# Cross attention with an RWKV block: recurrence over pairs of tokens, tail with channels on partitions, gate as silu on ScalarE

## The reference

```python
xa = _ln(x, ln1_w, ln1_b)
sx = concatenate([state[:, 1:2] - xa[:, :1], xa[:, :-1] - xa[:, 1:]], axis=1)
xxx = tanh((xa + sx * maa_x) @ maa_w1)            # five mixes of xa and sx from it
w = exp(-exp(time_decay + tanh(xw @ td_w1) @ td_w2))
r, k, v = xr @ Wr.T, xk @ Wk.T, xv @ Wv.T         # 32 heads of 16 channels
g = silu(xg @ Wg.T)
def step(s, rkvw):                                # over the 128 tokens
    a = k_t[..., :, None] * v_t[..., None, :]
    out = einsum('bhi,bhij->bhj', r_t, u * a + s)
    s = a + w_t[..., :, None] * s
og = (out - mean) / sqrt(var + 1e-05)             # per head
x1 = x + (og * gn_w + gn_b) * g @ Wo.T
# then a second layer norm and a channel mixing with Wfk, Wfr, Wfv on x1
```

## Time and profile before

| | |
|---|---|
| median of 3 runs | 1902.09 us (1901.77 to 1902.61) |
| the profiled execution's own time | 1903.22 us |
| its span | 1901.3 us |
| mean granted clock of TensorE | 0.976 of 2.4 GHz |
| TensorE, VectorE busy | 1761.4, 1775.5 us |
| ScalarE, GpSimd busy | 1196.1, 1253.3 us |

### The profile page before, as it was taken

The page is one execution under the profiler, slowest core; times in us unless marked ns, Lnnn a source line. Parts: engine busy times, 40 slices in busy tenths (PEclk is TensorE's granted clock), DMA queues, the critical chain, the costliest instruction groups (busy, mean ns, idle before and its releaser), DMA issues.

```text
span 1901.3 us, 34866 instructions
## 1 busy us (share of the span) xinstructions
PE 1761.4 (93%) x12356; PEld 1228.6 (65%) x12356; DVE 1775.5 (93%) x2084; ACT 1196.1 (63%) x2849; POOL 1253.3 (66%) x822
## 2 busy tenths in 40 slices
PE   5888999999999999999999999999999999999866
PEld 3666676767666677766667776666776666676533
DVE  3599999999999999999999999999999999999981
ACT  3546666666666666666666666666666666666422
POOL 1246777676777767677777766777776677776541
PEclk8899999999999999999999999999999999999878
DMA  6233433333343333333333443333443333333320
GB/s 239 60 98 96 106 102 92 101 104 102 100 106 99 92 101 104 104 101 102 99 91 102 106 106 98 103 98 91 105 107 103 98 103 96 95 107 96 91 66 11
DMA packets 86203, 189.32 MB, mean 100 GB/s; under 512 B 18800, under 2 KB 35312, under 8 KB 85008
## 3 DMA queue, kind: packets, MB, share of 16 engines
q1 hardware_dynamic: 64528, 170.32, 33.7%
q10 hardware_dynamic: 21504, 16.78, 2.7%
HBM read 161.91 MB, written 16.78 MB: 94 GB/s over the span
## 4 chain that ended last, share of the span: by engine, by line
DVE 52%; issue 24%; POOL 11%; PE 7%; ACT 6%; DVEq 0%; DMA 0%; POOLq 0%; ACTq 0%; SPq 0%
DVE S L615 18%; DVE S L606 8%; DVE S L624 8%; POOL rstd L402 7%; ACT wrep L863 3%; DVE xf L578 3%; PE bank L1004 3%; DVE nmax L521 3%; DVE xx L568 2%; PE bank L1011 1%; DVE xin L531 1%; POOL rstd L400 1%; DVE st L663 1%; DVE x L659 1%; POOL S L446 1%
## 5 line engine op out<-in xcount | busy, mean ns | idle before, releaser
L615 DVE TENSOR_TENSOR_SCAN S<-wrep,S 128x1024 f32<-128x1024 f32 x256 | 602.6, 2354 | 2.1 <-ACT wrep L863 0.8
L446 POOL COPY S<-s 128x8 f32<-128x8 f32 x256 | 281.4, 1100 | 291.9 <-PE bank L1129 283.3
L624 DVE TENSOR_TENSOR S<-S,rT 128x1024 f32<-128x1024 f32 x256 | 343.3, 1341 | 2.8 <-ACT rT L868 1.6
L606 DVE TENSOR_TENSOR S<-vrep,kT 128x1016 f32<-128x1016 f32 x256 | 341.0, 1332 | 0.0
L430 POOL TENSOR_TENSOR xf<-xf,xa 128x512 f32<-128x512 f32 x160 | 249.3, 1558 | 89.8 <-DVE xf L578 87.5
L402 POOL TENSOR_TENSOR rstd<-rstd,mhalf 128x1 f32<-128x1 f32 (+1 forms) x96 | 211.3, 2201 | 8.0
L1129 PE MATMUL bank<-S,slide 128*32 128x256 f32 x2048 | 165.0, 394 | 23.8 <-DVE S L624 23.7
L827 ACT ACTIVATE bank<-bank,par 128x128 f32<-128x128 f32 x640 | 175.8, 366 | 10.6 <-PE bank L1085 10.6
L402 POOL TENSOR_TENSOR hrs<-hrs,mhalf 128x32 f32<-128x32 f32 x32 | 174.8, 5462 | 2.7
L400 POOL TENSOR_SCALAR rstd<-mv 128x1 f32<-128x1 f32 (+1 forms) x96 | 36.2, 377 | 204.9 <-DVE mv L542 151.8
L790 ACT ACTIVATE prob<-bank,nmax 128x512 f32<-128x512 f32 x128 | 88.3, 690 | 102.4 <-DVE nmax L521 101.5
(11 more groups left out here) (131 smaller groups left out, 3763.3 us busy)
## 6 DMA issues: line engine op xcount, KB each, us to landing
vrep<-v_dram SPq DMA_DIRECT2D x256, 512.0 KB
xc<-x_c SPq DMA_DIRECT2D x32, 256.0 KB, 6.4
xs<-x_s SPq DMA_DIRECT2D x32, 256.0 KB, 7.1
v_dram<-vT ACTq DMA_DIRECT2D x32, 256.0 KB, 2.3
xres<-xin SPq DMA_DIRECT2D x32, 256.0 KB, 6.1
out<-rr ACTq DMA_DIRECT2D x32, 256.0 KB, 2.0
Wv<-big_w SPq DMA_DIRECT2D x1, 1024.0 KB, 7.3
Wk<-big_w SPq DMA_DIRECT2D x1, 1024.0 KB, 9.3
```

What stands on the lines that cost most here:

```text
L446: po.tensor_copy(S[:, u % 2, :, 0], s0[:, p, k:k + UJ]).then_inc(pool_wkv.sem, 1)
L606: ve_.tensor_tensor(S[:, u % 2, :, 1:P], vrep[:, u % 2, :, 0:P - 1], k, ALU.mult).then_inc(dve_wkv.sem, 1)
L615: ve_.tensor_tensor_scan(s, wrep[:, u % C, :, :].rearrange("p j t -> p (j t)"), s, 0.0, ALU.mult, ALU.add).then_inc(dve_wkv.sem, 1)
L624: ve_.tensor_tensor(s, s, rT[:, p, u % C, :].unsqueeze(1).broadcast_to([P, UJ, P]), ALU.mult).then_inc(dve_wkv.sem, 1)
```

## The change

1. **Pairs of tokens.** With s(t+2) = w w' s(t) + (w' a + a'), the scan goes over the state before every even token: 64 per row in place of 128. Into k of the even tokens goes the next token's decay (`mid_kw`), into r of the odd tokens the even token's decay (`mid_rw`); `wkv_pair` adds the two products; the read multiplies each state with both tokens' r. The even token's own product, which the odd token's output needs, goes in through a second bonus: r of the odd with k of the even token (`wkv_rk2`), summed per head on TensorE (`tail_C`) and multiplied with the even token's v (`tail_o2`, `tail_ob`). GpSimd multiplies the two decays (`mid_ez2`); ScalarE computes w once (`mid_w`), and `decay` becomes a repeated copy of 504 elements per chunk.
2. **Tail with channels on partitions.** The columns of Wv and Wg and the rows of Wo are reordered on the host, so that the sums of the recurrence lie like v and the gate. `tail_To` and `tail_Tg` and the copy of the sums go; `tail_os` adds the sums to the bonus from PSUM. The variance is a product with a block of ones (`tail_Vr`), epsilon is added on ScalarE (`tail_hv`), the power stays on GpSimd, its result is repeated (`tail_hp`), transposed (`tail_Rs`), and multiplied in from PSUM (`tail_gn`).
3. **Gate.** `mid_th` is silu from its bank, `mid_gate` goes. The activations need more than one function table, so loads of a table are placed between them.
4. **Around it.** xin has three buffers and the copy to xres goes. v is stored by four transfers. The back jobs have three banks. kT and rT lose their second buffer, kt and rt have two. All five orders are new.

```diff
+            def mid_ez2(n, m, p):
+                eng.wait_ge(act_mid.sem, act_mid.count("dw", n))
+                eng.wait_ge(act_decay.sem, act_decay.count("w3", n - 1))
+                po.tensor_tensor(ez2[:, :, :], first(ez[:, :, :]), second(ez[:, :, :]), ALU.mult).then_inc(pool_ez2.sem, 1)
...
+            def wkv_rk2(n, m, p):
+                eng.wait_ge(act_mid.sem, act_mid.count("r", n))
+                eng.wait_ge(pe_tail.sem, pe_tail.count("C", n - 1))
+                po.tensor_tensor(rk2[:, :, :], second(rT[:, :, :]), first(kT[:, :, :]), ALU.mult).then_inc(pool_rk2.sem, 1)
...
+                ve_.tensor_tensor(first(kt[:, p, :, :]), first(kT[:, :, :]), second(ez[:, :, :]),
+                                  ALU.mult).then_inc(dve_pre.sem, 1)
...
+                k = kt[:, p, u % C, 0:P - 2].unsqueeze(1).broadcast_to([P, UJ, P - 2])
+                ve_.tensor_tensor(A[:, u % 2, :, 0:P - 2], vrep[:, u % 2, :, 0:P - 2], k, ALU.mult).then_inc(dve_outer.sem, 1)
+
+            def wkv_pair(n, m, p, u):
+                eng.wait_ge(dve_outer.sem, dve_outer.count(f"a{u}", n))
+                a = A[:, u % 2, :, 0:P - 2]
+                ve_.tensor_tensor(S[:, u % 2, :, 1:T2], first(a), second(a), ALU.add).then_inc(dve_pair.sem, 1)
...
+                out4 = A[:, u % 2, :, :].rearrange("p j (m k) -> p j m k", k=2)
+                s = S[:, u % 2, :, :].unsqueeze(3).broadcast_to([P, UJ, T2, 2])
+                r = rt[:, p, u % C, :].rearrange("p (m k) -> p m k", k=2).unsqueeze(1).broadcast_to([P, UJ, T2, 2])
+                ve_.tensor_tensor(out4, s, r, ALU.mult).then_inc(dve_read.sem, 1)
...
+            def tail_os(n, m, p):
+                eng.wait_ge(dve_tail.sem, dve_tail.count("ob", n))
+                eng.wait_ge(pe_wkv.sem, pe_wkv.count(f"r{U - 1}", n))
+                ve_.tensor_tensor(oc[:, :], bank[SUM_BANK][:, :], oc[:, :], ALU.add).then_inc(dve_tail.sem, 1)
...
+                for g in range(P // H):
+                    eng.dma_start(rows[g], vT[H * g:H * (g + 1), p, :, :]).then_inc(v_stored, 16)
...
-                sc.activation(wrep[:, c, :, 1:P], ez[:, c, 0:P - 1].unsqueeze(1).broadcast_to([P, UJ, P - 1]),
-                              ACT.Exp, scale=-1.0).then_inc(act_decay.sem, 1)
+                sc.activation(wrep[:, c, :, 1:T2], ez2[:, c, 0:T2 - 1].unsqueeze(1).broadcast_to([P, UJ, T2 - 1]),
+                              ACT.Copy).then_inc(act_decay.sem, 1)
...
-                sc.activation(gT[:, p, :, :], by_chunk(bank_of("G")[:, :]), ACT.Tanh, scale=0.5).then_inc(act_mid.sem, 1)
+                sc.activation(gT[:, p, :, :], by_chunk(bank_of("G")[:, :]), ACT.Silu).then_inc(act_mid.sem, 1)
...
+                for c in range(C):
+                    last = pe.matmul(bank_of("C")[:, P:P + T2], heads_of[:, c, :], rk2[:, c, :],
+                                     start=(c == 0), stop=(c == C - 1))
...
+            def tail_Vr(n, m, p):
+                eng.wait_ge(act_tail.sem, act_tail.count("sq", n))
+                eng.wait_ge(*bank_free("Vr", n))
+                for c in range(C):
+                    last = pe.matmul(bank_of("Vr")[:, 0:H], sq[:, c * P:(c + 1) * P], head_sum[:, :],
+                                     start=(c == 0), stop=(c == C - 1))
```

More of the change, by code:

```diff
@@ L31 @@
 U = C * HS // UJ
-CONSTS = 14 + C
+T2 = P // 2
+CONSTS = 16 + 3 * C
 LAGS = 5
@@ L179, in by_chunk, with first, second @@
             return ap.rearrange("p (c t) -> p c t", c=C)
+        def first(ap):
+            return ap.rearrange("p c (m k) -> p c m k", k=2)[:, :, :, 0]
+        def second(ap):
+            return ap.rearrange("p c (m k) -> p c m k", k=2)[:, :, :, 1]
         xn = prob[:, 0, :]
@@ L549, in centre_wv @@
                 eng.wait_ge(setup_loaded[2], 16 * len(BIG))
-                wv = W["Wv"][:, :, :].rearrange("p c (h j) -> p (c h) j", j=HS)
-                total = sx[:, 0, :]
+                wv = W["Wv"][:, :, :].rearrange("p c (j h) -> p c h j", j=HS)
+                total = sx[:, 0, :].rearrange("p (c h) -> p c h", c=C)
                 ve_.tensor_reduce(total, wv, X, ALU.add).then_inc(wv_centred, 1)
                 eng.wait_ge(wv_centred, 1)
-                ve_.scalar_tensor_tensor(wv, total.unsqueeze(2).broadcast_to([P, C * H, HS]), -1.0 / HS, wv,
-                                         ALU.mult, ALU.add).then_inc(wv_centred, 1)
+                for c in range(C):
+                    last = ve_.scalar_tensor_tensor(wv[:, c, :, :], total[:, c, :].unsqueeze(2).broadcast_to([P, H, HS]),
+                                                    -1.0 / HS, wv[:, c, :, :], ALU.mult, ALU.add)
+                last.then_inc(wv_centred, 1)
                 eng.wait_ge(wv_centred, 2)
@@ new lines, in tail_ob @@
+            def tail_ob(n, m, p):
+                eng.wait_ge(dve_tail.sem, dve_tail.count("o2", n))
+                b2 = second(by_chunk(oc[:, :]))
+                ve_.tensor_tensor(b2, b2, pv[:, :, :], ALU.add).then_inc(dve_tail.sem, 1)
+            def tail_os(n, m, p):
+                eng.wait_ge(dve_tail.sem, dve_tail.count("ob", n))
+                eng.wait_ge(pe_wkv.sem, pe_wkv.count(f"r{U - 1}", n))
+                ve_.tensor_tensor(oc[:, :], bank[SUM_BANK][:, :], oc[:, :], ALU.add).then_inc(dve_tail.sem, 1)
@@ L755, in step @@
-                if b1: wkv_outer(*b1, 0)
             run(step)
@@ L1149, in tail_To, with tail_Rs @@
                 for c in range(C):
-                    last = pe.matmul(bank[O_BANK][:, c * P:(c + 1) * P], bonus[:, c * P:(c + 1) * P], ident[:, :],
-                                     start=False, stop=(c == C - 1), is_transpose=True)
+                    last = pe.matmul(bank_of("Vr")[:, 0:H], sq[:, c * P:(c + 1) * P], head_sum[:, :],
+                                     start=(c == 0), stop=(c == C - 1))
                 last.then_inc(pe_tail.sem, 1)
-            def tail_Tg(n, m, p):
-                eng.wait_ge(dve_tail.sem, dve_tail.count("o3", n))
-                eng.wait_ge(*bank_free("Tg", n))
-                transposes("Tg", lambda c: oc[:, c * P:(c + 1) * P]).then_inc(pe_tail.sem, 1)
+            def tail_Rs(n, m, p):
+                eng.wait_ge(act_tail.sem, act_tail.count("hp", n))
+                eng.wait_ge(*bank_free("Rs", n))
+                pe.transpose(bank_of("Rs")[:, 0:P], hrep[:, :], ident[:, :]).then_inc(pe_tail.sem, 1)
```

483 lines of the change are left out of this document (263 added, 220 removed).

## The result

The changed kernel took 1906.7 us, median of 10 runs (1905.4 to 1911.2), beside 1901.9 for the kernel before on the same chip: ratio 1.0029, 95% interval 1.0019 to 1.0039. It is slower by 0.3%, where 1882 was forecast. The profiled execution took 1906.4 us; its span is 3.4 us longer than that of the kernel before.

A forecast was written before the change was run, and what follows sets the result against it. VectorE was taken to bound the kernel before, TensorE after the change. Thirty periods at 0.59 us gave 18 us, the ends 2, the profiled execution 1: 1903.2 - 20 - 1 = 1882 us, range 1855 to 1926.

The forecast's parts named there:

- TensorE's work: TensorE per period: transposes out, bonus and variance products in, 53.82 to 53.95 us (53.7 to 54.6), becoming the bound.
- VectorE's need: VectorE per period: recurrence saves 3.9 us, the rest adds 0.7, so 55.1 falls to 51.9 us; port meetings add 0 to 2.
- Table switch: Two table loads per batch; the one at the tanh behind W1, 1.28 us, idles TensorE 0.93 us each period.
- My sign of being wrong: Forecast wrong if TensorE's work falls under 53 us, the second load stands elsewhere, or the steady granted clock leaves 1.00.
- the first one's: Rival 1: switch costs TensorE nothing (load ahead of the wait, or silu's table holds tanh); period 54.2, 1858 us; chance 0.20.
- The period: Steady stretch: TensorE's 53.95 us plus 0.93 idle plus 0.1 other waits make 55.0 us, against 55.59 before.
- Rival 3: VectorE waits for GpSimd's copies or a sum two units before, outgrowing 3.1 us slack; period 55.6, 1900 us; chance 0.13.
- Sum -2: Ramp and drain: last batch's recurrence saves 4 us, its tail 1; constants and centring add 2 to 4; net -2 us.
- the stores of v: Four store issues on ScalarE's queue counted as nothing; if their cover failed, a batch's first product would wait some 2 us.
- longer constants and the centring: At the start, longer constants and a strided centring of Wv add 2 to 4 us.
- It sets the period: Kernel before: VectorE, busy 55.13 of 55.66 us and idle 0.53, sets the period; TensorE stands 1.8 us behind.
- the 1 us that I took off for the profiled execution: Final sum: the profiled execution, 1903.2 us, stood 1.1 above the runs' median of 1902.1, so 1 us came off.

The follow-up runs named there:

- run 1: Changed kernel with tanh in place of silu for the gate, so all activations share one table: 1907.4 us, ratio 1.0028 to the kernel before.
- run 2: Changed kernel with the gate's product moved ahead of pair sum 4 in VectorE's order: 1907.5 us, ratio 1.003 to the kernel before.
- run 9: Changed kernel with a third product buffer and VectorE's read 0 moved ahead of scan 1: 1886.0 us, ratio 0.9916 to the kernel before.
- run 13: Changed kernel with a third product buffer, plus one semaphore wait so outer product 2 waits for read 1: 1887.9 us, ratio 0.9930 to the kernel before.
- run 4: Changed kernel with v stored by one transfer in the old layout, output not the reference's: 1901.9 us, ratio 1.0007 to the kernel before.
- run 3: Changed kernel with the once-per-run centring of Wv moved behind the first mid_xx: 1898.7 us, ratio 0.9984 to the kernel before.
- run 12: Kernel before with only the silu gate taken over, one 512-element VectorE instruction gone, two table loads a period: 1898.7 us, ratio 0.9975.
- run 14: Changed kernel with three product buffers, early read 0 and later centring (1877.0 us), plus a wait ahead of outer product 2: 1882.3 us, ratio 0.9905.
- run 5: Changed kernel with a third product buffer, so outer product 2 no longer waits for sum 0: 1968.9 us, ratio 1.0358 to the kernel before.

## Why the prediction was wrong

- **TensorE's work: right.** 53.95 was forecast, 54.0 measured, with some luck. The 64-column products took 0.12 us an instruction and the 32-column ones 0.11, 1.85 us in all for my 1.35: fewer columns saved nothing. Jobs that I had left as they were took 0.4 us less and covered it.
- **VectorE's need: nearly.** 51.9 was forecast, 52.7 measured, within the 0 to 2 us left for meetings at the port. Stepped operands ran at full rate (a pair sum of 504 took 0.67 us, a plain operation over 512 the same). VectorE does not wait for GpSimd's copies, as I had expected, but for TensorE's sums (30.5 us in 23.5 periods).
- **Table switch: wrong, and its two errors do not meet.** I put the second load ahead of the tanh behind W1 and the idle time at 0.93 us. There is no load there, and TensorE does not wait there (run 1: 1907.4 with no switch at all). My sign of being wrong, a second load that stands elsewhere, came. Of my rivals' conditions, the first one's held, that silu's table has tanh; its time did not follow.
- **The period: 55.22 for 55.0, near by luck.** In place of the 0.93 us behind W1 TensorE waits 1.03 us for the gate. It is held by a loop: two product buffers tie outer product 2 to sum 0 on TensorE (0.97 us); from there VectorE's stretch, prolonged by GpSimd, leads back to TensorE (run 2: the wait only changes its place; runs 9 and 13: with the tie gone and GpSimd let through, the period is 54.6). Rival 3 named this mechanism, a product waiting for the sum of two units before, but let it decide only beyond 3.1 us of slack. Slack as a difference of two sums is not slack in a loop.
- **The ends: the step that failed.** "Sum -2" was +14 (15.2 - 1.2). I set the stores of v at nothing; run 4 puts them at 3.3 to 4.8 us, through a wait of 1.90 us in the first steps. I set longer constants and the centring at 2 to 4 us; W1 starts 3.2 us later, which is that, but the ramp passes more on than it takes in: in run 3 W1 came 5.1 us earlier and the end 8.0. By that measure the two explain some 7 to 10 of the 14 us. The rest is open. TensorE's new wait of 2.83 us for the copy of v, which no term of mine had, is a candidate; no run tested the new order of the first steps. I priced the instructions and did not follow who waits behind them where no other batch's work lies in between.
- **"It sets the period" for the kernel before: too quick.** 55.13 of 55.66 us busy, yet run 12 took 0.60 us of VectorE's work away with no effect on the period. The 0.37 us a period that the whole change brought, with 2.4 us less on VectorE, say the same.

In numbers: the periods brought 10.6 us and not 18 (7.4), and the ends are off by 16. With the 1 us that I took off for the profiled execution and the 0.4 by which the median stands above it now, that is 24.8, the 24.7 us between 1882 and 1906.7.

## What to carry to other kernels

Price a change to a pipelined kernel at its ends as carefully as in its steady stretch: walk through the first step queue by queue, because there a moved setup instruction can lie on the path whole. When an engine is nearly full, ask in which loop its waits lie (buffer, producer, consumer) before taking the difference of two sums for slack. And before closing a gap on VectorE, look at what small GpSimd instruction ends in it; if one does, try a short wait there and measure it. The wait brought 81 us in run 13 and cost 5 in run 14, where nothing was held up.

## What the runs showed of the hardware that I had not expected

- GpSimd's copy of eight elements took 4.46 us under five VectorE instructions that overlap at their edges, and 1.03 us where VectorE's queue had a break; one added semaphore wait is worth 81 us (runs 5 and 13).
- A table load costs its 1.28 us and no drain where activations are queued ahead of it (gaps of 0.01 to 0.03 us in 47 loads), and it runs ahead of its activation's wait when the table changes at that instruction, other than the first load of the program. The Trainium skill, "ScalarE: Activation LUTs", section "What ACT_TABLE_LOAD costs", counts 1.38 us more per switch; the trace does not agree, and the measurement decides.
- Four stores of a quarter each of v kept ScalarE's queue for 2.5 us, where one took 0.4 (run 4).
- Eight TensorE instructions with 64 moving columns took 0.117 us each and eight with 32 took 0.113; with 128 columns they took 0.110 to 0.124 (changed kernel, start to start).
